# First layer's convolution on 64-row tiles, and the column fold on GpSimd, in a Fourier-operator kernel

## The reference

```python
h = jnp.concatenate([grid, x], axis=-1) @ P_w + P_b      # 5 -> 32 channels
for i in range(4):
    h_ft = jnp.fft.rfft2(h)
    out_modes = einsum('bixy,ioxy->boxy', h_ft[:, :, :16, :16], w_c[i])
    spec = jnp.fft.irfft2(out_modes, s=(64, 64))
    conv = conv_3x3(h, conv_w[i]) + conv_b[i]
    h = leaky(spec + conv)
tokens = leaky(h @ Q1_w + Q1_b) @ Q2_w + Q2_b
...
```

## Time and profile before

| | us |
|---|---|
| median of three runs | 7531.51 |
| lowest and highest | 7525.21, 7532.25 |
| the profiled execution | 7536.45 |
| its span, first to last instruction | 7534.4 |
| TensorE busy in the span | 6726.4 (89%) |
| VectorE busy | 4995.7 (66%) |
| ScalarE busy | 2567.0 (34%) |
| GpSimd busy | 61.3 (1%) |

### The profile page before, as it was taken

How to read it: one execution, slowest core, us unless ns; L and a number is a source line. 1 busy time by engine, 2 the same in 40 slices (tenths; PEclk the granted TensorE clock), 3 DMA queues, 4 the chain that set the end, 5 groups by cost and what they waited for, 6 DMA issues and landing times. The chain is left out here.

```text
span 7534.4 us, 262144 instructions
## 1 busy us (share of the span) xinstructions
PE 6726.4 (89%) x107382; PEld 3991.5 (53%) x107382; DVE 4995.7 (66%) x7931; ACT 2567.0 (34%) x4418; POOL 61.3 (1%) x47
## 2 busy tenths in 40 slices
PE   5699998999999899999989999758888888888888
PEld 4466666666666666666654444334434444344443
DVE  3599995777777477777667777664545555455454
ACT  1244442333333233333223333233343333433333
POOL 1000000000000000000000000000000000000000
PEclk8899998999999899999999999879999999999999
DMA  6444444444444444444432222200000000000000
GB/s 155 113 124 129 125 124 134 125 124 118 123 124 110 138 118 124 124 118 123 117 100 77 77 76 75 86 6 1 3 1 3 3 1 3 2 2 3 1 3 2
DMA packets 655549, 568.39 MB, mean 75 GB/s; under 512 B 328096, under 2 KB 527904, under 8 KB 649126
## 3 DMA queue, kind: packets, MB, share of 16 engines
q1 hardware_dynamic: 655176, 563.43, 28.2%
HBM read 315.77 MB, written 247.61 MB: 75 GB/s over the span
## 5 line engine op out<-in xcount | busy, mean ns | idle before, releaser
L548 PE MATMUL abank<-inv_basis,mode_tile 128*32 128x128 f32 x32768 | 1013.6, 276 | 94.6 <-DMA mode_tile<-m_img 66.4
L594 PE MATMUL zbank<-rows_in,conv_taps 64*32 64x512 f32 (+1 forms) x18432 | 1049.7, 588 | 0.0
L548 PEld LDWEIGHTS abank<-inv_basis,mode_tile 128*32 128x32 f32 x32768 | 877.3, 111 | 269.4 <-issue 269.4
L954 DVE SCALAR_TENSOR_TENSOR rows_out<-zbank,conv_bias,work 128x1024 f32<-128x1024 f32 x512 | 633.7, 1279 | 516.9 <-PE zbank L603 504.9
L816 ACT ACTIVATE turned<-tbank 128x1024 f32<-128x1024 f32 x400 | 410.2, 1026 | 1550.9 <-PE tbank L617 1550.9
L810 ACT ACTIVATE inv_copy<-abank 128x1024 f32<-128x1024 f32 x512 | 524.4, 1024 | 776.4 <-PE abank L548 776.4
L632 PE MATMUL zbank<-fwd_basis,turned 128*64 128x128 f32 x12288 | 760.2, 277 | 19.9 <-ACT turned L816 13.1
L930 DVE TENSOR_TENSOR work<-inv_copy 128x512 f32<-128x512 f32 x1024 | 653.6, 684 | 164.1 <-ACT inv_copy L810 163.8
L632 PEld LDWEIGHTS zbank<-fwd_basis,turned 128*64 128x64 f32 x12288 | 668.6, 137 | 97.7 <-issue 97.7
L603 PE MATMUL zbank<-rows_in,conv_taps 32*32 32x512 f32 (+1 forms) x18432 | 702.5, 593 | 0.0
L594 PEld LDWEIGHTS zbank<-rows_in,conv_taps 64*32 64x32 f32 x18432 | 329.5, 106 | 583.0 <-issue 583.0
(11 more groups left out here) (367 smaller groups left out, 7091.2 us busy)
## 6 DMA issues: line engine op xcount, KB each, us to landing
h_rows<-rows_out SPq DMA_DIRECT2D x768, 256.0 KB, 4.1
rows_in<-h_rows SPq DMA_DIRECT2D x384, 512.0 KB, 4.9
m_img<-rows_out SPq DMA_DIRECT2D x32, 1024.0 KB, 5.3
mode_tile<-m_img SPq DMA_DIRECT2D x512, 64.0 KB, 3.1
rows_in<-x_pad SPq DMA_DIRECT2D x384, 48.7 KB
rows_out<-x_pad SPq DMA_DIRECT2D x384, 48.7 KB
tokens<-spectra SPq DMA_DIRECT2D x512, 4.0 KB
weights<-in_weights SPq DMA_DIRECT2D x1, 6060.0 KB, 19.5
```

What stands on the lines that cost most here:

```text
L548: last = nc.tensor.matmul(ab[32 * p:32 * p + 32, s, 128 * k:128 * k + 128], mode_tile[u][:, k, a, :], inv[:, k, s, 128 * p:128 * p + 128], ...
L594: nc.tensor.matmul(section(zb[32 * p:32 * p + 32, 2 * a + so, :])[:, :, :, out], conv_t[part, dx, so, :], moving(part, p, 0, src), start=( ...
L954: nc.vector.scalar_tensor_tensor(out=rows_out[u][:, half].rearrange("p (s x) -> p s x", s=2), in0=zb[:, 2 * a:2 * a + 2, :], scalar=conv_b ...
```

## The change

In the first layer each parity gets its own 54 rows (3 shifts dx of 3 rows of 3 image and 3 grid channels): parity 0 on partitions 0 to 53, parity 1 on 64 to 117. A product has 54 rows, held by a 64-row tile, and 32 columns, and the two parities of an image are issued in turn. Image 0 goes first, then the wait for `g_ready`, then image 1. A row used by both parities is now loaded twice. In every layer but the last the column fold of a pair runs on GpSimd, which has a loop of its own for it; the eight folds of the embedding ahead of the layers stay on VectorE.

```diff
-            for s in range(2):
-                if s == 1:
+            for a in range(2):
+                if a == 1:
                     pe.wait_ge(g_ready, ET + n - 1)
                     pe.nop(nofuse=True)
-                for a in range(2):
-                    planes_of = x_rows[u][:, a, 0:J * PITCH].rearrange("p (h q j w) -> p q h j w", h=2, q=4, w=PITCH)
-                    for p in range(4):
-                        last = nc.tensor.matmul(section(zb[32 * p:32 * p + 32, 2 * a + s, :]), x_conv[:, 32 * s:32 * s + 32],
-                                                planes_of[:, p, :, :, 0:COLS], start=True, stop=True)
+                planes_of = x_rows[u][:, a, 0:J * PITCH].rearrange("p (h q j w) -> p q h j w", h=2, q=4, w=PITCH)
+                for p in range(4):
+                    for s in range(2):
+                        part = slice(64 * s, 64 * s + 54)
+                        last = nc.tensor.matmul(section(zb[32 * p:32 * p + 32, 2 * a + s, :]), x_conv[part, :],
+                                                planes_of[part, p, :, :, 0:COLS], start=True, stop=True)
...
         def sp_grid_rows(sp, u):
             for dx in range(3):
-                at = 32 * dx + 12
-                sp.dma_start(x_rows[u][at:at + 12, :, 0:SPAN],
-                             grid_slots.rearrange("r k x -> (r k) x")[:, dx:dx + SPAN].unsqueeze(1).broadcast_to([12, 2, SPAN])).then_inc(grid_rows_in[u], 16)
+                for s in range(2):
+                    at = 64 * s + 18 * dx + 9
+                    sp.dma_start(x_rows[u][at:at + 9, :, 0:SPAN],
+                                 grid_slots[s:s + 3, :, dx:dx + SPAN].rearrange("r k x -> (r k) x").unsqueeze(1).broadcast_to([9, 2, SPAN]))\
+                        .then_inc(grid_rows_in[u], 16)
 
         def sp_x_rows(sp, u, n):
             for dx in range(3):
-                for r in range(4):
-                    at, start = 32 * dx + 3 * r, ROW_START[r] + dx
-                    sp.dma_start(x_rows[u][at:at + 3, :, 0:SPAN],
-                                 x_pad[bass.ds(2 * n, 2), ROW_SET[r], :, start:start + SPAN].rearrange("a c x -> c a x"))\
+                for s in range(2):
+                    at = 64 * s + 18 * dx
+                    alone, both = (at, at + 3) if s == 0 else (at + 6, at)
+                    start = (0, 2 * PITCH)[s] + dx
+                    sp.dma_start(x_rows[u][alone:alone + 3, :, 0:SPAN],
+                                 x_pad[bass.ds(2 * n, 2), 1 - s, :, start:start + SPAN].rearrange("a c x -> c a x"))\
+                        .then_inc(x_rows_in[u], 16)
+                    sp.dma_start(x_rows[u][both:both + 6, :, 0:SPAN],
+                                 x_pad[bass.ds(2 * n, 2), :, :, PITCH + dx:PITCH + dx + SPAN].rearrange("a r c x -> (r c) a x"))\
                         .then_inc(x_rows_in[u], 16)
...
+            def fold_cols(g):
+                pool.wait_ge(rows_folded, g + 1)
+                pool.nop(nofuse=True)
+                v = by_row[:].rearrange("p x (j v w) -> p (x j) v w", v=2, w=COLS // 2)
+                for y, op in ((0, ALU.add), (1, ALU.subtract)):
+                    need(pool, flip_done, 2 * g + y - 1)
+                    nc.gpsimd.tensor_tensor(folded[:, y, :, :, :].rearrange("p x b (j w) -> p (x b j) w", w=COLS // 2),
+                                            v[:, :, 0, :], v[:, :, 1, :], op).then_inc(cols_folded, 1)
+
+            with looped(pool, 0, PAIRS) as n:
+                fold_cols(ET + n)
+            with pool.Fori(1, LAST) as l:
+                with looped(pool, 0, PAIRS) as n:
+                    fold_cols(ET + PAIRS * l + n)
...
                 next_inverse(1)
-                fold_cols(ET + layers + n)
                 if not is_last(n):
                     spectral_rows(n + 1 + layers)
```

More of the change, by code:

```diff
@@ L103, in build_tokenizer @@
         expand_bd = sb("expand_bd", [128, 64])
-        embed_t = sb("embed_t", [128, 32])
-        x_conv = sb("x_conv", [128, 64])
-        conv_bd = sb("conv_bd", [128, 3, 64])
+        embed_t = sb("embed_t", [128, 90])
+        x_conv = sb("x_conv", [128, 32])
+        conv_bd = sb("conv_bd", [128, 3, 32])
         conv_t = sb("conv_taps", [128, 3, 3, WID])
@@ L183, in build_tokenizer @@
         NP = PAIRS // 2
-        NZERO = ET + 2 + 8
+        NZERO = ET + 2 + 7
         LAST = LAYERS - 1
@@ L285, in sp_late_constants @@
             column = lambda ap: ap.rearrange("(c o) -> c o", o=1)
-            part, at = slice(32 * r, 32 * r + 32), 3 * r
+            part, at = slice(32 * r, 32 * r + 32), 36 + 3 * r
             loads = 0
@@ L291, in load @@
                 loads += 1
[L292 to L296, removed]
+            if r < 3:
+                for k in range(3):
+                    load(embed_t[part, at + k:at + k + 1], column(embed_w[2 + k, :]))
+                for k in range(2):
+                    load(embed_t[part, at + 9 + k:at + 10 + k], column(embed_w[k, :]))
+                load(embed_t[part, at + 11:at + 12], column(embed_b))
             load(q1_bias[part, :], column(q1_b))
@@ L303, in sp_late_constants @@
             if r == 1:
[L304 to L310, removed]
+                for dy in range(3):
+                    load(conv_bd[32 * dy:32 * dy + 32, :, :], conv_w[0, dy, :, :, :].rearrange("c x o -> c x o"))
+            assert loads == (11, 12, 9, 3)[r]
+        NLATE = 11 + 12 + 9 + 3
         def sp_grid_modes(sp):
@@ L527, in _ @@
             nc.gpsimd.memset(embed_t[:], 0.0).then_inc(zeroed, 1)
-            nc.gpsimd.memset(x_conv[:], 0.0).then_inc(zeroed, 1)
             nc.gpsimd.memset(q2_bd[:], 0.0).then_inc(zeroed, 1)
@@ L558, in pe_x_conv @@
             if isinstance(n, int) and n < 2:
-                pe_need(pe, grid_rows_in[u], 48)
-            for s in range(2):
-                if s == 1:
+                pe_need(pe, grid_rows_in[u], 96)
+            for a in range(2):
+                if a == 1:
                     pe.wait_ge(g_ready, ET + n - 1)
                     pe.nop(nofuse=True)
-                for a in range(2):
-                    planes_of = x_rows[u][:, a, 0:J * PITCH].rearrange("p (h q j w) -> p q h j w", h=2, q=4, w=PITCH)
-                    for p in range(4):
-                        last = nc.tensor.matmul(section(zb[32 * p:32 * p + 32, 2 * a + s, :]), x_conv[:, 32 * s:32 * s + 32],
-                                                planes_of[:, p, :, :, 0:COLS], start=True, stop=True)
+                planes_of = x_rows[u][:, a, 0:J * PITCH].rearrange("p (h q j w) -> p q h j w", h=2, q=4, w=PITCH)
[4 more added lines that the diff above has]
+                                                planes_of[part, p, :, :, 0:COLS], start=True, stop=True)
             last.then_inc(z_done, 1)
@@ L788, in _ @@
             pe.nop(nofuse=True)
-            for dx in range(3):
-                last = nc.tensor.matmul(ab[32 * dx:32 * dx + 32, 0, 0:64], embed_t[:], conv_bd[:, dx, :],
-                                        start=True, stop=True)
+            for s in range(2):
+                for dx in range(3):
+                    last = nc.tensor.matmul(ab[64 * s:64 * s + 54, 0, 0:32], embed_t[0:96, 36 - 18 * dx:90 - 18 * dx],
+                                            conv_bd[0:96, dx, :], start=(dx == 0), stop=(dx == 2))
             last.then_inc(x_conv_done, 1)
@@ L907, in layer @@
                     act.wait_ge(x_conv_done, 1)
-                    nc.scalar.activation(x_conv[0:96, :], ab[0:96, 0, 0:64], ACT.Identity).then_inc(x_conv_ready, 1)
+                    for s in range(2):
+                        part = slice(64 * s, 64 * s + 54)
+                        last = nc.scalar.activation(x_conv[part, :], ab[part, 0, 0:32], ACT.Identity)
+                    last.then_inc(x_conv_ready, 1)
                 run(kind, l)
```

## The result

The changed kernel takes 7675.54 us (four runs, 7668.03 to 7688.36) against 7531.88 (7525.21 to 7545.0) for the kernel before beside it: ratio 1.0185, 95% interval 1.0171 to 1.0198. That is 144 us slower, where 7547 was forecast within a range of 7476 to 7705. The time lies in the range, at the place of the slow rival (7692), not of the forecast.

The account below looks back on a forecast made before the run. VectorE and TensorE were taken to bound the first layer at about 14.1 us per pair. First-layer periods +8, layer ends +4 and start +3 made +15 on 7536.45, or 7551.5; as a median 7547 us, range 7476 to 7705.

Parts of the forecast that it names:

- the slow rival: First layer: both GpSimd instructions run in a row before VectorE is let in; period 16.67 us, 7692 us in all; chance 0.28.
- Two bounds at 14.1: First layer: VectorE and TensorE both want about 14.1 us per pair, so easing one alone gives next to nothing.
- Part 1: First layer's x convolution on 64-row tiles: eight share the array, a half takes 1.00 us, TensorE's period falls 14.10 to 13.25.
- The start: Kernel start: a mode load queued behind the larger row loads comes later, +3 us, bounds 0 and 6.
- P: Time of one GpSimd column fold instruction of 128x1024 with two SBUF inputs: 2.4 us, bounds 1.2 to 2.85.
- That the engines hold one another: First layer: VectorE's two-input SBUF runs hold GpSimd off, and GpSimd's fold holds VectorE for P.
- Who stands behind whom: First layer: spectral rows wait for the first GpSimd instruction only; the second runs beside the next pair's new rows.
- 11.87 + P: VectorE's first-layer period after the change: 14.27 us, +0.13 per pair, +8 us over 61 periods.
- Middle layers: Middle layers: VectorE's 3.65 us wait per pair covers the hold, 1.1 remains; no change in time.
- Layer ends: Three layer ends where nothing covers the fold: TensorE gets the first half 1.3 us later at each, +4 us.
- both rivals: First layer: no mutual hold (7484 us, chance 0.32), and both GpSimd instructions in a row (7692 us, chance 0.28).

Follow-up runs that it names:

- experiment 1: The changed kernel with the column fold back on VectorE, keeping the 64-row tiles and wider row loads: ratio 1.0004 against the kernel before.
- experiment 7: The kernel before, old convolution and loads, with only half the column fold on GpSimd beside the new rows: ratio 1.0009 against the kernel before.
- experiment 3: The changed kernel with GpSimd's two fold adds replaced by four memsets, which read nothing: 7482.87 us, ratio 0.9914 against the kernel before.
- experiment 4: The changed kernel with half the fold back on VectorE, GpSimd's half released by the next pair's spectral rows: 7496.94 us, ratio 0.9933 against the kernel before.
- experiment 5: As experiment 4, without the wait for the spectral rows, GpSimd's half released by the row fold at once: ratio 0.9966 against the kernel before.
- experiment 2: The kernel before with only the column fold moved to GpSimd, convolution and row loads unchanged: ratio 1.0175 against the kernel before.
- experiment 6: The changed kernel with GpSimd's two adds replaced by two copies that read one SBUF input: ratio 0.994 against the kernel before.

## Why the prediction was right or wrong, point by point

**Two bounds at 14.1.** Right. Experiments 1 and 7 each ease one of them and leave the time where it was.

**Part 1.** Right in its steady state. A half is 16 records in 1.09 against 1.92 and takes 1.02 to 1.07 from its start to the flip (1.00 was worked out), the wait for the copy of the modes 1.56 (1.57 was worked out), TensorE's period 13.28 in experiment 3 (13.25). The start, for which 3 was taken between 0 and 6, is not settled: the third new rows come 1.4 us (experiment 3) to 5.8 us (experiment 1) later than in the trace before, but with the old loads they come 4.1 earlier in experiment 7, so that starts differ by as much without the wider loads.

**GpSimd's price.** P = 2.4 was taken between 1.90 and 2.85; undisturbed, in experiment 4, it is 2.39 on average (53 instructions of 2394 ns). The estimate of 2.25 from the Trainium skill, GPSIMD Engine Reference, "Performance versus the Vector engine", was a little low; the measurement decides.

**That the engines hold one another.** Right, in both directions. The reading of the one place in the old trace, 2.83 against 1.63, was right that VectorE's unbroken run keeps GpSimd out: experiment 5's 6.58 shows the same. The other direction, which that trace hardly showed, is as strong: 3.24 for a spectral row of 1.22. The Trainium skill, SBUF — State Buffer, "Who interferes with whom", said so for both orders, and for writes that they don't contend; the traces agree with it on all three (3.24, 6.58, and 1225 ns beside memsets). But it is not always the instruction issued first that goes first: in experiment 5 L1027, L975 and L976 started after GpSimd's record did, and all three ran before its work.

**Who stands behind whom: the step that failed.** The prediction said: "spectral rows stand behind the first GpSimd instruction (P), go next, and the second GpSimd instruction runs beside the new rows of the next pair (2.39 against 2.4)". After the first GpSimd instruction only the first of the two spectral rows went; then the second GpSimd instruction had its turn, and the second spectral row stood behind that. So both P were paid, not one: the place and time of the slow rival, with another order inside (it had both GpSimd instructions in a row). By its sum the period would be 16.67; measured are 16.20 in the first kind and 16.75 in the second, 16.39 on average. In the first kind VectorE stands for 2.02 and 2.17 us (3.24 and 3.39 less 1.22 each), less than P both times. The term of the sum that fell is 11.87 + P; the one that holds is nearly 11.87 + 2P. I had drawn from the four instructions of the earlier trace rows that VectorE's runs are never broken. They are: GpSimd's first instruction gets in at about 813.2, where the spectral rows wait for their own input, as predicted, and its second between L965 and L966, where no gap of VectorE is recorded.

**Middle layers.** Right: TensorE stays at 200 of 200. VectorE's inverse sums stand there for GpSimd, too (5.32 for a pair at 1711.12, 1.28 before), and its wait for the convolution shrank from 3.65 to 1.77 per pair, where 1.1 was left by the working. The 1.4 us per layer are small but real: the middle layers take 1148.26 in experiment 2 too, and 1146.9 to 1147.4 in every run without the whole fold on GpSimd; 1.2 of them fall on the layer's first two pairs (33.08 against 31.90).

**Layer ends.** +4 was taken for three of them; from the last new rows to the next layer's first it is 120.07, 118.04 and 117.24 against 118.61, 122.34 and 120.03, not more in sum. TensorE does wait for GpSimd's fold there (0.69 at 1321.72), but a load of spectral weights behind it (`in_spec_uv`) takes that up: VectorE waits for it until 23.9 us after the last new rows in both kernels, 9.09 us in place of 10.84. This term was not there.

**The range and the chances.** The range of 7476 to 7705 was drawn to reach both rivals, so that the time falls in it bears out nothing of the forecast's mechanism. That the slow rival's 7692 came near is in part luck: its order of turns was wrong, and its sum held because either order costs two GpSimd instructions. The slow rival had 0.28 and the forecast 0.36, though the trace before had no row for GpSimd reading at length beside VectorE. What would have told the two apart was to follow the turns instruction by instruction with GpSimd's second instruction already waiting: nothing in the old trace said that VectorE's next instruction goes before it.

## What to carry to other kernels

Work moved from VectorE to GpSimd comes back as VectorE's own time if GpSimd reads SBUF while VectorE runs instructions with two SBUF inputs: here two instructions of 1.13 us each were taken off and up to 2.2 us each came back as standing time. Before moving it, look for a stretch in which VectorE reads PSUM and at most one SBUF operand, at least as long as GpSimd's instruction, and release GpSimd there by a semaphore; the same 2.4 us instruction was free there (experiment 4) and cost 2.1 us where it got in between two such instructions (experiment 5). And where two engines are within 1% of one another, ease both, or expect nothing.

## What the runs showed of the hardware

- A GpSimd record shows its waiting as work: the same subtract is 2.39 us beside the new rows and 6.58 us behind a run of VectorE instructions. Likewise a VectorE record of 3.24 us is 1.22 of work.
- What decides whether GpSimd gets into a run of VectorE instructions is not settled. One reading fits all pairs of experiment 5: it is kept out while VectorE goes on without a gap (44 first-layer pairs, and the middle layers' first pairs), and gets in behind the next instruction where VectorE had just paused (18 pairs). It fits the changed kernel's turns as well, where GpSimd gets in between L965 and L966 after L965 had stood. It does not fit the layer's first pair in the changed kernel (287.47) and in experiments 2 and 6, where GpSimd got in behind an inverse sum that had followed the row fold at once. No experiment changed the gap alone.
- An instruction with a single SBUF input tensor can be held as well: at the first layer's end VectorE's sign product (two of 64x512, SBUF to SBUF, by a column of signs) takes 2.90 us beside GpSimd, 0.93 before. The second and third layer's ends show the same, and so do those of experiment 2.

```profile
1318.85 2.90 DVE L1105 TENSOR_SCALAR uv<-uv,sign 64x512 f32<-64x512 f32 x2
1318.93 5.03 POOL L547 TENSOR_TENSOR folded<-by_row 128x1024 f32<-128x1024 f32 x2 [8.73 <-DVE by_row L997]
```

- TensorE, waiting 2.87 us for VectorE at 821.44, did the next forward transform in 3.06 us in place of 1.97, at a mean granted clock of 0.96 in the layer (1.00 before): part of it at 1.2 GHz in place of 2.4. It is not the bound there, but a late inverse copy lets GpSimd go first (829.05). All 61 periods agree with this: in the 22 of 16.70 to 16.81 that forward transform has a part at 1.2 GHz and takes 2.7 us or more, and the inverse copy ends 8.7 us or more after the new rows' start, later than GpSimd's start at 8.5; in the 39 of 16.13 to 16.25 the transform takes 1.97 and the copy ends at 7.4. By the two means, 22 times 0.55, about 12 of the 137 us come this way (an estimate).
